# A decoder layer on one core: two batches' Silu by Tanh ahead of the last cross softmax, the last batch in halves, context means early, new orders

## The chip, the cores and the metric

The kernel runs on one core of one Trainium2 chip. The metric is device time in microseconds (us) of one execution; a run's time is a little more than the span that the profiler sees. TensorE (PE) multiplies matrices and transposes, VectorE (DVE) and ScalarE (ACT) work on what it leaves in PSUM, GpSimd (POOL) on SBUF alone, and SyncE (SP) issues DMAs. The engines run at the same time and wait for each other by semaphores.

## What is computed

```python
x = x + attn(layernorm(x), Wq, bq, Wk, bk, Wv, bv, Wo, bo)   # causal, 4 KV heads, rope, d = 16
x = x + xattn(layernorm(x), ctx_2048, mask_BxS2_bk0)         # softmax(x @ ctx.T / 16) @ ctx, masked
x = x + ffn(layernorm(x), w_gate_up, w_down)
# ffn: everything is quantised to 255 steps per row and multiplied back
#   gate, up = quantised(x) @ quantised(w_gate_up).T, split in halves of 704
#   h = silu(gate) * up;  y = quantised(h) @ quantised(w_down).T
```

x is 8 batches of 128 tokens with 256 features; the context is 8 x 128 x 256. The reference's einsum of the scores sums over the 4 query heads of a KV head, so the kernel sums the columns of Wq beforehand.

## The kernel before

One batch is one tile of 128 tokens. For each batch j of 8 the steps are small functions, one call a step: `project` (q, k, v in bank `ps_q`), `rotate` and `rotate_sum` (rope, DVE, with `rotate_c` on POOL), `transpose_qk`, `mask_scores` and `scores` (bank group `ps_s`), `max_scores`, `transpose_q_max`, `mask_other_keys` and `score_keys` (scores transposed, with the row maximum folded in), `exp_self` (ACT), `weigh_values` (`ps_y`), `invert_sums`, `normalise_y`, `project_out`, `residual_1`; then the cross attention: `transpose_x1`, `cross_scores` (`ps_x`), `max_cross`, `bias_cross`, `exp_cross`, `transpose_cross_p`, `readout` (`ps_r`), `residual_2`; then the feed-forward part: `quantise_x`, `transpose_x_int`, `gate_product` (8 matmuls of 352 columns into banks 0 and 1 of `ps_s`), `silu_gate` (ACT), `widen_gate` (POOL: times the scales of the up weights), `up_product` (banks 2 and 3), `hidden` (DVE: up times gate), `amax_h`, `scale_h`, `invert_h`, `quantise_h` (ACT), `transpose_h` (`ps_x`), `evacuate_h`, `down` (`ps_y`), `scale_down` (DVE), `add_residual` (POOL; DVE for the last batch) and the store.

Beside the batches there is work that is done once: the mean over the columns of the weights (`mean_w_first`, `centre_w_first`), bias under rope (`sum_bias`, `rope_bias`, DVE), Wo with bias centred (`bias_wo` on PE, `sum_wo`, `mean_wo`, `centre_wo` on DVE), the token means of the context (`mean_ctx`), the quantisation of the weights (`amax_w1`, `amax_w2`, `quantise_w1`, `quantise_w2`), and the transposes of gate, up and down weights by way of bank `ps_r`. The gate weight is kept as an upper and a lower part (`gate_hi`, `gate_lo`), whose sum has full precision. `keep_warm(n)` are n matmuls on zeros whose result nobody reads.

There is no scheduler. Each engine has one list of calls, written out by hand, and runs it in that order; a wait that is not yet met holds back all that follows on that engine. `done(engine, name, j)` waits until semaphore `name` has counted batch j, `bank_free` and `free` wait until a buffer or bank is read out. So a product into the gate banks waits for the Silu of the batch before:

```python
bank_free(pe, "gate_ready", j)      # gate_product(j) waits for silu_gate(j - 1)
```

Silu needs another set of ACT's function tables than Exp, so the list of ACT has every `exp_cross` ahead of the first `silu_gate`.

## Time and profile before

| | us |
|---|---|
| median of 3 runs | 111.41 |
| lowest and highest | 111.39, 113.15 |
| the profiled execution | 111.01 |
| its span | 109.2 |
| PE busy in the span | 96.1 |
| DVE, ACT, POOL busy | 75.5, 64.7, 60.2 |

Times below are us from the start of the span of the profiled execution. Busy time of PE counts modelled ends of matmuls, so that a full PE is not one at its peak. "PEclk" or the granted clock is the share of the full clock of 2.4 GHz that PE was given; 0.50 is its lower level of 1.2 GHz.

### The profile page before, as it was taken

The page shows a single profiled execution, that of the slowest core. Times are in us where ns is not written, and L with a number is a line of the kernel's source. Part 1 is how long each engine was busy: PE and PEld are TensorE (multiplying, and loading weights), DVE is VectorE, ACT ScalarE, POOL GpSimd, SP SyncE. Part 2 cuts the span into 40 slices and gives each one's busy share as a digit, 9 for nine tenths or more (in the row PEclk, how much of TensorE's full clock was granted, in tenths as well). Part 3 has the DMA queues.
Part 4 walks back from the last instruction along what each step waited for, and adds up shares of the span by engine and source line. Part 5 has one row for each costly group of instructions (what it writes and reads, how often), then busy time and mean ns, then how long its engine had stood idle before and what let it go on. Part 6 is the DMA issues. An engine that isn't in the chain of part 4 may idle for free.

```text
span 109.2 us, 2451 instructions
## 1 busy us (share of the span) xinstructions
PE 96.1 (88%) x827; PEld 74.7 (68%) x827; DVE 75.5 (69%) x216; ACT 64.7 (59%) x169; POOL 60.2 (55%) x122
## 2 busy tenths in 40 slices
PE   6998396999999999999999998766799999999850
PEld 4786284799876677687688786445687888865520
DVE  5176939978669695956984846367698868889331
ACT  1300113870859748686668493889877587788620
POOL 6364402999358994135162143255888968765430
PEclk9999959985599999999999999999999999999999
DMA  2999999700000000000000000000000000111212
GB/s 53 382 331 405 417 420 388 230 0 0 0 9 0 0 0 3 6 0 0 0 6 0 0 0 0 9 0 0 0 0 0 0 0 6 51 48 48 96 54 96
DMA packets 4522, 8.35 MB, mean 76 GB/s; under 512 B 349, under 2 KB 3358, under 8 KB 4382
## 3 DMA queue, kind: packets, MB, share of 16 engines
q1 hardware_dynamic: 4206, 7.64, 19.2%
q10 hardware_dynamic: 304, 0.56, 1.4%
q8 instruction: 7, 0.11, 0.5%
q14 instruction: 5, 0.04, 0.1%
HBM read 7.15 MB, written 1.05 MB: 75 GB/s over the span
## 4 chain that ended last, share of the span: by engine, by line
PE 71%; DVE 12%; ACT 6%; DMA 4%; issue 3%; ACTq 1%; DVEq 0%
PE ps_s L447 15%; PE ps_q L295 7%; PE ps_r L281 5%; PE ps_y L486 5%; DMA mask_sb<-in_mask 4%; PE ps_s L343 3%; PE ps_y L363 3%; PE ps_r L390 3%; PE ps_s L319 3%; PE ps_x L379 3%; PE ps_x L474 3%; PE ps_q L303 2%; PE ps_y L355 2%; PE ps_s L330 2%; PE ps_s L314 2%
## 5 line engine op out<-in xcount | busy, mean ns | idle before, releaser
L1029 POOL TENSOR_TENSOR gate_up<-gate,up_row 128x704 f32<-128x704 f32 x8 | 13.6, 1700 | 3.0 <-ACT gate L645 2.9
L255 PE MATMUL ps_s<-warm 128*128 128x256 bf16 x51 | 9.4, 361 | 1.0 <-DVE warm L679 1.0
L1041 POOL TENSOR_SCALAR x_aug<-x2c 128x256 f32<-128x256 f32 x8 | 3.8, 480 | 10.5 <-DVE x2c L832 10.4
L540 ACT ACTIVATE v_pad<-ps_q,r 128x64 f32<-128x64 f32 x8 | 2.5, 314 | 11.9 <-DVE rot L781 11.9
L804 DVE RECIPROCAL y_rsum<-ps_y 128x128 f32<-128x128 f32 x8 | 7.6, 953 | 2.3 <-PE ps_y L358 2.1
L645 ACT ACTIVATE gate<-ps_s,x_scale 128x704 f32<-128x704 f32 x8 | 6.8, 847 | 3.9 <-PE ps_s L447 3.9
L901 DVE SCALAR_TENSOR_TENSOR hid<-ps_s,x_scale,gate_up 128x704 f32<-128x704 f32 x8 | 7.6, 949 | 1.7 <-PE ps_s L447 1.4
L255 PEld LDWEIGHTS ps_s<-warm 128*128 128x128 bf16 x51 | 6.5, 131 | 3.2 <-DVE warm L679 1.0
L447 PE MATMUL ps_s<-gate_hi,x_int_T 128*128 128x352 f32 x32 | 8.4, 343 | 0.0
L1007 POOL TENSOR_TENSOR rot_c<-rot,b_rope 128x128 f32<-128x128 f32 x8 | 3.6, 455 | 8.5 <-DVE rot L781 8.5
L486 PE MATMUL ps_y<-w_T,h_T 128*128 128x256 bf16 (+1 forms) x48 | 7.5, 276 | 0.6 <-DVE ffn L920 0.6
L447 PE MATMUL ps_s<-gate_lo,x_int_T 128*128 128x352 f32 x32 | 7.8, 323 | 0.0
L650 ACT ACTIVATE h_int<-hid,h_inv 128x704 int16<-128x704 f32 x8 | 7.0, 881 | 1.0 <-PE ps_x L474 0.8
L799 DVE TENSOR_REDUCE qk_rot<-ps_s 128x4 f32<-128x512 f32 x8 | 5.5, 690 | 2.7 <-PE ps_s L319 2.7
L1056 POOL TENSOR_TENSOR y_out<-ffn,x_aug 128x256 f32<-128x256 f32 x7 | 4.8, 690 | 4.4 <-DVE ffn L920 4.4
L781 DVE TENSOR_TENSOR rot<-ps_q,rope_r 128x256 f32<-128x256 f32 x8 | 3.4, 422 | 5.5 <-PE ps_q L295 5.3
L906 DVE TENSOR_REDUCE h_amax<-hid 128x1 f32<-128x704 f32 x8 | 7.0, 876 | 0.1
L920 DVE SCALAR_TENSOR_TENSOR ffn<-ps_y,h_scale,w_row 128x256 f32<-128x256 f32 x8 | 3.9, 482 | 4.5 <-PE ps_y L486 4.3
L447 PE MATMUL ps_s<-up_int,x_int_T 128*128 128x352 f32 x32 | 7.0, 339 | 0.0
L390 PE MATMUL ps_r<-ctx_aug,p_cross_T 128*128 128x257 f32 x16 | 5.2, 407 | 1.6 <-ACT x_int_T L631 0.7
L638 ACT CAST h_T<-ps_x 128x640 bf16<-128x640 int16 x8 | 5.5, 685 | 1.7 <-PE ps_x L474 1.7
L486 PEld LDWEIGHTS ps_y<-w_T,h_T 128*128 128x128 bf16 (+1 forms) x48 | 4.0, 97 | 3.4 <-issue 1.7
(165 smaller groups left out, 282.2 us busy)
## 6 DMA issues: line engine op xcount, KB each, us to landing
w_raw<-in_w SPq DMA_DIRECT2D x2, 512.0 KB, 9.5
ctxT<-in_ctxT SPq DMA_DIRECT2D x1, 1024.0 KB, 12.3
ctx_aug<-in_ctx SPq DMA_DIRECT2D x1, 1024.0 KB, 15.6
out_x<-y_out SPq DMA_DIRECT2D x8, 128.0 KB, 1.7
x_aug<-in_x SPq DMA_DIRECT2D x1, 768.0 KB, 7.4
xT<-in_xT SPq DMA_DIRECT2D x1, 768.0 KB, 8.6
w_raw<-in_w SPq DMA_DIRECT2D x1, 704.0 KB, 13.6
x_first<-in_x_first ACTq DMA_DIRECT2D x1, 416.0 KB, 5.6
```

Of the source, the lines that this page charges most:

```text
L255: nc.tensor.matmul(ps_s[:, H - 1, 0:2 * T], warm[:, 0:P], warm[:, :], start=True, stop=True)
L295: last = nc.tensor.matmul(ps_q[:, 0:6 * QK], x_feature(j, c), wqkv_c[:, c, :, :], start=c == 0, stop=c == DC - 1)
L390: nc.tensor.matmul(ps_r[:, 0:DA], p_cross_T[:, j, :], ctx_aug[:, j, :], start=True, stop=True).then_inc(s["readout_done"], 1)
L447: last = nc.tensor.matmul(ps_s[:, first + i, 0:FH], x_int_T[:, j, c, :], w[:, c, i * FH:(i + 1) * FH], start=c == 0 and w is parts[0], sto ...
L486: last = nc.tensor.matmul(ps_y[:, 0:D], h_T[j % 2][0:n, f, :], w2_T[0:n, f, :], start=f == 0, stop=f == FC - 1)
L638: nc.scalar.copy(h_T[j % 2][:, 0:FC - 1, :], src[:, 0:(FC - 1) * T].rearrange("p (f t) -> p f t", t=T))
L645: nc.scalar.activation(gate[j % 2][:, :, :], ps_s[:, 0:2, 0:FH], ACT.Silu, scale=x_scale[:, j:j + 1]).then_inc(s["gate_ready"], 1)
L650: nc.scalar.mul(h_int[j % 2][:, :], hid[j % 2][:, :, :].rearrange("p i f -> p (i f)"), h_inv[:, j:j + 1]).then_inc(s["h_int_ready"], 1)
L804: nc.vector.reciprocal(y_rsum[j % 3][:, :], ps_ys).then_inc(s["y_rsum_done"], 1)
L901: nc.vector.scalar_tensor_tensor(hid[j % 2][:, :, :], ps_s[:, 2:4, 0:FH], x_scale[:, j:j + 1], gate_up[j % 2][:, :, :], ALU.mult, ALU.mult ...
L906: nc.vector.tensor_reduce(h_amax[:, j:j + 1], hid[j % 2][:, :, :].rearrange("p i f -> p (i f)"), AX.X, ALU.max, apply_absolute_value=True) ...
L1029: nc.gpsimd.tensor_tensor(gate_up[j % 2][:, :, :], gate[j % 2][:, :, :], up_row[:, :].rearrange("p (i f) -> p i f", i=2), ALU.mult).then_i ...
```

## The change

**Silu by Tanh.** For batches 0 and 1 (`EARLY = 2`) silu(g) is computed as g/2 · (1 + tanh(g/2)): ACT takes the tanh from the gate bank (`tanh_gate`), DVE adds 1 and multiplies by the bank (`finish_gate`), and `hidden` uses the scale squared and halved (`x_square`), which POOL computes with `x_half`. A gate product waits for what reads its bank for the batch before: `finish_gate` (batches 0 and 1) or the Silu, which now counts from batch 2 (`gate_free`). **Last batch in halves.** Gate product, Silu, widening (now DVE), `hidden`, maximum, quantisation, transposes, evacuation and `down` of batch 7 go by halves (columns 0 to 351 and the rest for the first steps, 384 and 320 for the quantised ones). The other transposes of h alternate between banks `ps_x` and `ps_q`. **Context means.** `ctxT` is loaded before `xT` and w1; `mean_ctx` comes before the first keys are scored, and each of its 16 matmuls writes 60 equal columns in place of 1 (`CM = 61`). **Elsewhere.** The bias goes to POOL (the key bias is copied by ACT), Wo's centring to ACT, `x_first` is loaded by SP and `wo` by ACT. All four lists of calls are written in another order; that the diff shows only in a line or two of each.

```diff
             sp.dma_start(w_first[:, :], w_first_in).then_inc(s["w_first_loaded"], 16)
+            sp.dma_start(x_first[:, :], x_first_in).then_inc(s["x_first_loaded"], 16)
             sp.dma_start(x_second[:, :], x_second_in).then_inc(s["x_second_loaded"], 16)
-            sp.dma_start(wo_raw[:, :], wo_in).then_inc(s["wo_loaded"], 16)
             sp.dma_start(x_aug[:, 2:B, 0:D], x_in).then_inc(s["x_loaded"], 16)
+            sp.dma_start(ctxT[:, :, :, :], ctxT_in).then_inc(s["ctxT_loaded"], 16)
             sp.dma_start(xT[:, :, :, :], xT_in).then_inc(s["xT_loaded"], 16)
             for part, (first, last) in enumerate(W1_PARTS):
                 sp.dma_start(w1_raw[:, first:last, :], w1_in[:, first:last]).then_inc(s[f"w1_{part}_loaded"], 16)
-            sp.dma_start(ctxT[:, :, :, :], ctxT_in).then_inc(s["ctxT_loaded"], 16)
...
-                    nc.tensor.matmul(ps_s[:, H - 1, 0:2 * T], warm[:, 0:P], warm[:, :], start=True, stop=True)
+                    nc.tensor.matmul(ps_r[:, 0:2 * T], warm[:, 0:P], warm[:, :], start=True, stop=True)
...
+                means = ps_r[:, 0:B * CM].rearrange("p (b n) -> p b n", n=CM)
+                nc.tensor.matmul(means[:, :, 0], mean_w[0:B, :], any_diag[:, :], start=True, stop=True)
                 pe.wait_ge(s["ctxT_loaded"], 16)
                 for j in range(B):
                     for c in range(DC):
-                        last = nc.tensor.matmul(ps_r[:, B + j:B + j + 1], ctxT[:, j, c, :], mean_w[:, 0:1],
+                        last = nc.tensor.matmul(means[:, j, 1:CM], ctxT[:, j, c, :], mean_w[:, 1:CM],
                                                 start=c == 0, stop=c == DC - 1)
                 last.then_inc(s["ctx_mean_done"], 1)
...
+            def gate_free(j):
+
+                if 1 <= j <= EARLY:
+                    pe.wait_ge(s["early_gate_ready"], j)
+                elif j > EARLY:
+                    pe.wait_ge(s["gate_ready"], j - EARLY)
+
             def gate_product(j):
                 if j == 0:
                     done(pe, "p_T_ready", B - 1)
                     done(pe, "gate_lo_ready", 2)
-                bank_free(pe, "gate_ready", j)
+                gate_free(j)
...
+            def last_gate(i):
+
+                if i == 0:
+                    gate_free(LAST)
+                    done(pe, "x_int_T_ready", LAST)
+                for c in range(DC):
+                    for w in (gate_hi, gate_lo):
+                        last = nc.tensor.matmul(ps_s[:, i, 0:FH], x_int_T[:, LAST, c, :], w[:, c, i * FH:(i + 1) * FH],
+                                                start=c == 0 and w is gate_hi, stop=c == DC - 1 and w is gate_lo)
+                last.then_inc(s["last_gate_done"], 1)
...
             def transpose_h(j):
+
+                bank = (ps_x, ps_q)[j % 2]
                 if j == 0:
                     done(pe, "cross_p_T_ready", B - 1)
-                bank_free(pe, "h_T_ready", j)
+                elif j == 1:
+                    done(pe, "qk_T_ready", B - 1)
+                free(pe, "h_T_ready", j, 2)
                 done(pe, "h_int_ready", j)
```

```diff
+            def last_down_a():
+
+                done(pe, "ffn_ready", LAST - 1)
+                done(pe, "last_h_T_a_ready", 0)
+                for f in range(FC // 2):
+                    nc.tensor.matmul(ps_y[:, 0:D], h_T[LAST % 2][:, f, :], w2_T[:, f, :], start=f == 0, stop=False)
+
+            def last_down_b():
+
+                done(pe, "last_h_T_b_ready", 0)
+                for f in range(FC // 2, FC):
+                    n = P if f < FC - 1 else FL
+                    last = nc.tensor.matmul(ps_y[:, 0:D], h_T[LAST % 2][0:n, f, :], w2_T[0:n, f, :],
+                                            start=False, stop=f == FC - 1)
+                last.then_inc(s["down_done"], 1)
...
-            keep_warm(30); mean_w_first(); keep_warm(6); project(0); bias_wo(); keep_warm(10); transpose_qk(0)
-            keep_warm(5); project(1); mask_scores(0); scores(0); transpose_q_max(0); mask_other_keys(0)
...
+            keep_warm(30); mean_w_first(); keep_warm(6); mask_scores(0); bias_wo(); keep_warm(4); project(0)
+            keep_warm(11); transpose_qk(0); project(1); scores(0); keep_warm(7); mean_ctx(None, 0)
+            transpose_q_max(0); mask_other_keys(0); score_keys(0); transpose_qk(1); project(2)
...
+            def copy_key_bias():
+                act.wait_ge(s["x_first_loaded"], 16)
+                nc.scalar.copy(b_qk[:, :, QK:2 * QK], b_raw[:, :, QK * G:]).then_inc(s["bias_copied"], 1)
+
+            def centre_wo():
+
+                done(act, "wo_biased", 0)
+                nc.scalar.activation(y_out[:, 0, :], ps_y[:, 0:D], ACT.Identity, scale=-1.0 / D, accum_out=wo_negmean[:, :]).then_inc(s["wo_summed"], 1)
+                done(act, "wo_summed", 0)
+                nc.scalar.activation(wo_aug[:, 0:D], ps_y[:, 0:D], ACT.Identity, bias=wo_negmean[:, 0:1])
+                nc.scalar.mul(wo_aug[:, D:DA], wo_negmean[:, :], -1.0).then_inc(s["wo_ready"], 1)
...
+            def tanh_gate(j):
+
+                done(act, "x_half_ready", j)
+                done(act, "gate_done", j)
+                nc.scalar.activation(gate[j % 2][:, :, :], ps_s[:, 0:2, 0:FH], ACT.Tanh, scale=x_half[:, j:j + 1]).then_inc(s["tanh_done"], 1)
...
+            def last_silu(i):
+                done(act, "gate_up_ready", LAST - 2)
+                done(act, "x_scale_ready", LAST)
+                done(act, "last_gate_done", i)
+                nc.scalar.activation(gate[LAST % 2][:, i, :], ps_s[:, i, 0:FH], ACT.Silu, scale=x_scale[:, LAST:B]).then_inc(s["last_gate_ready"], 1)
```

```diff
+            def finish_gate(j):
+
+                done(dve, "tanh_done", j)
+                nc.vector.scalar_tensor_tensor(gate[j % 2][:, :, :], gate[j % 2][:, :, :], 1.0, ps_s[:, 0:2, 0:FH],
+                                               ALU.add, ALU.mult).then_inc(s["early_gate_ready"], 1)
+
+            def last_widen(i):
+
+                done(dve, "hid_ready", LAST - 2)
+                done(dve, "last_gate_ready", i)
+                nc.vector.tensor_tensor(gate_up[LAST % 2][:, i, :], gate[LAST % 2][:, i, :], up_row[:, i * FH:(i + 1) * FH],
+                                        ALU.mult).then_inc(s["last_gate_up_ready"], 1)
+
+            def last_hidden(i):
+                done(dve, "h_int_ready", LAST - 2)
+                done(dve, "up_done", LAST)
+                done(dve, "last_gate_up_ready", i)
+                nc.vector.scalar_tensor_tensor(hid[LAST % 2][:, i, :], ps_s[:, 2 + i, 0:FH], x_scale[:, LAST:B], gate_up[LAST % 2][:, i, :],
+                                               ALU.mult, ALU.mult).then_inc(s["last_hid_ready"], 1)
+
+            def last_amax_h(i):
+                done(dve, "last_hid_ready", i)
+                nc.vector.tensor_reduce(last_amax[:, i:i + 1], hid[LAST % 2][:, i, :], AX.X, ALU.max,
+                                        apply_absolute_value=True).then_inc(s["last_amax_done"], 1)
+
...
+                if j < EARLY:
+                    done(dve, "x_square_ready", j)
+                scale = x_square[:, j:j + 1] if j < EARLY else x_scale[:, j:j + 1]
+                nc.vector.scalar_tensor_tensor(hid[j % 2][:, :, :], ps_s[:, 2:4, 0:FH], scale, gate_up[j % 2][:, :, :],
...
-            sum_bias(); rope_bias(); rope_bias_sum(); centre_w_first(); stats_1(1); aggregate_1(1, 2)
-            sum_wo(); mean_wo(); centre_wo(); rotate(0); stats_1(2); exclude(); rotate_sum(0); stats_1(3)
...
+            finish_gate(0); invert_sums(7); residual_2(5); amax_x(5); normalise_y(7); step_x(5); invert_x(5)
+            max_cross(6); bias_cross(6); finish_gate(1); residual_1(7); hidden(0); amax_h(0)
+            scale_h(0); invert_h(0); max_cross(7); bias_cross(7); invert_cross_sum(6); hidden(1); residual_2(6)
```

```diff
+            def sum_bias():
+
+                pool.wait_ge(s["x_first_loaded"], 16)
+                nc.gpsimd.tensor_tensor(bq_half[:, :, :, :], bq_raw[:, :, :, 0:2], bq_raw[:, :, :, 2:4], ALU.add).then_inc(s["bias_half_summed"], 1)
+                done(pool, "bias_half_summed", 0)
+                nc.gpsimd.tensor_tensor(b_qk[:, :, 0:QK], bq_half[:, :, :, 0], bq_half[:, :, :, 1], ALU.add).then_inc(s["bias_summed"], 1)
+
+            def rope_bias():
+                done(pool, "bias_summed", 0)
+                done(pool, "bias_copied", 0)
+                nc.gpsimd.tensor_tensor(b_cos[:, :, :], b_qk[:, :, :], rope_sb[:, 0:2, :], ALU.mult).then_inc(s["b_cos_done"], 1)
+                nc.gpsimd.tensor_tensor(b_sin[:, :, :], b_qk[:, ::-1, :], rope_sb[:, 3:1:-1, :], ALU.mult).then_inc(s["b_sin_done"], 1)
+                done(pool, "b_cos_done", 0)
+                done(pool, "b_sin_done", 0)
+                nc.gpsimd.tensor_tensor(b_rope[:, :, :], b_cos[:, :, :], b_sin[:, :, :], ALU.add).then_inc(s["b_rope_ready"], 1)
...
+                if j < EARLY:
+                    done(pool, "early_gate_ready", j)
+                else:
+                    done(pool, "gate_ready", j - EARLY)
...
+                    done(pool, "x_scale_ready", j)
+                    nc.gpsimd.tensor_scalar(x_half[:, j:j + 1], x_scale[:, j:j + 1], 0.5, 1.0, ALU.mult, ALU.mult).then_inc(s["x_half_ready"], 1)
+                    nc.gpsimd.tensor_scalar(x_square[:, j:j + 1], x_scale[:, j:j + 1], x_scale[:, j:j + 1], 0.5, ALU.mult, ALU.mult).then_inc(s["x_square_ready"], 1)
```

**Order on PE at the context means.** First before: `weigh_values(0)` (two rows), `scores(1)`, the means (`ps_r<-mean_w,ctxT`) and `transpose_q_max(1)` (`ps_s<-ident,qk_rot`) with what follows it.

```order
L355 MATMUL ps_y<-p_self_T,v_pad 32x128 x4
L358 MATMUL ps_y<-p_self_T,ones 32x128 x4
L319 MATMUL ps_s<-qk_T 128x128 x4
L277 MATMUL ps_r<-any_diag,mean_w 128x8
L281 MATMUL ps_r<-mean_w,ctxT 128x1 x16
L325 MATMUL ps_s<-ident,qk_rot 128x128
L330 MATMUL ps_s<-causal_T,ident_b 128x128 x3
L303 MATMUL ps_q<-ident,qk_rot 128x128 x2
```

Now, from `project(1)` and `scores(0)` (`ps_s<-qk_T`) on:

```order
L304 MATMUL ps_q<-wqkv_c,x_second 128x192 x2
L328 MATMUL ps_s<-qk_T 128x128 x4
L263 MATMUL ps_r<-warm 128x256 x7
L286 MATMUL ps_r<-any_diag,mean_w 128x8
L290 MATMUL ps_r<-mean_w,ctxT 128x60 x16
L334 MATMUL ps_s<-ident,qk_rot 128x128
L339 MATMUL ps_s<-causal_T,ident_b 128x128 x4
L352 MATMUL ps_s<-q_max_T,qk_T 128x128 x4
L312 MATMUL ps_q<-ident,qk_rot 128x128 x2
```

The means moved up by one batch, from ahead of `transpose_q_max(1)` to ahead of `transpose_q_max(0)`, behind seven warm matmuls.

**Order on PE at the last cross steps.** `gate_hi`, `gate_lo`, `up_int` are products of the feed-forward part, `ps_x<-ctxT,x1c_T` is `cross_scores`, `ps_r<-ctx_aug,p_cross_T` a `readout`. Before, from `project_out(7)` to the last `transpose_cross_p`:

```order
L363 MATMUL ps_y<-wo_aug,y_T 128x257
L410 MATMUL ps_r<-ident_b,w_int 128x128 x6
L384 MATMUL ps_x<-ident,p_cross 128x128
L390 MATMUL ps_r<-ctx_aug,p_cross_T 128x257
L369 MATMUL ps_x<-ident,x1c 128x128 x2
L447 MATMUL ps_s<-up_int,x_int_T 128x352 x4
L377 MATMUL ps_x<-excluded,ident_b 128x128
L379 MATMUL ps_x<-ctxT,x1c_T 128x128 x2
L438 MATMUL ps_r<-ident_b,x_int 128x128 x2
L390 MATMUL ps_r<-ctx_aug,p_cross_T 128x257
L384 MATMUL ps_x<-ident,p_cross 128x128
```

Now, the same stretch, from `project_out(7)` on:

```order
L372 MATMUL ps_y<-wo_aug,y_T 128x257
L393 MATMUL ps_x<-ident,p_cross 128x128
L447 MATMUL ps_r<-ident_b,x_int 128x128 x2
L378 MATMUL ps_x<-ident,x1c 128x128 x2
L456 MATMUL ps_s<-gate_hi,x_int_T 128x352 x2
L456 MATMUL ps_s<-gate_lo,x_int_T 128x352 x2
L456 MATMUL ps_s<-gate_hi,x_int_T 128x352 x2
L456 MATMUL ps_s<-gate_lo,x_int_T 128x352 x2
L386 MATMUL ps_x<-excluded,ident_b 128x128
L388 MATMUL ps_x<-ctxT,x1c_T 128x128 x2
L456 MATMUL ps_s<-up_int,x_int_T 128x352 x4
L399 MATMUL ps_r<-ctx_aug,p_cross_T 128x257
```

`gate_product(2)` and `up_product(1)` now stand here, and `gate_product(1)` and `up_product(0)` ahead of the first row; before, `gate_product(1)` and all that follow it stood behind the last `transpose_cross_p`.

**Order on ACT there.** Before, the last `exp_cross` (`p_cross,c_sum`), the table load and the first Silu (`gate<-ps_s,x_scale`):

```order
L627 ACTIVATE x_int<-x2c,x_inv 128x256
L631 CAST x_int_T<-ps_r 128x256
L573 ACTIVATE p_cross,c_sum<-ps_x,c_bias,c_scale 128x128
L645 ACT_TABLE_LOAD
L645 ACTIVATE gate<-ps_s,x_scale 128x704
L578 COPY p_cross_T<-ps_x 128x128
L582 ACTIVATE y_out,x_sumsq<-x2c 128x256
```

Now, with the two Tanh (`gate<-ps_s,x_half`) among the cross exponentials, and the table load:

```order
L641 ACTIVATE p_cross,c_sum<-ps_x,c_bias,c_scale 128x128
L732 ACTIVATE gate<-ps_s,x_half 128x704
L646 COPY p_cross_T<-ps_x 128x128
L679 CAST up_int<-ps_r 128x3x2x128
...
L732 ACTIVATE gate<-ps_s,x_half 128x704
L641 ACTIVATE p_cross,c_sum<-ps_x,c_bias,c_scale 128x128
...
L749 ACTIVATE h_int<-hid,h_inv 128x704
L641 ACTIVATE p_cross,c_sum<-ps_x,c_bias,c_scale 128x128
L738 ACT_TABLE_LOAD
L738 ACTIVATE gate<-ps_s,x_scale 128x704
```

The Tanh of batches 0 and 1 stand ahead of `exp_cross(6)`; no table load stands between them and the exponentials. The first Silu, still behind the last `exp_cross`, is that of batch 2.

**Order on DVE at the end.** Before, from `hidden(7)` on:

```order
L901 SCALAR_TENSOR_TENSOR hid<-ps_s,x_scale,gate_up 128x704
L920 SCALAR_TENSOR_TENSOR ffn<-ps_y,h_scale,w_row 128x256
L906 TENSOR_REDUCE h_amax<-hid 128x1
L911 TENSOR_SCALAR h_scale<-h_amax 128x1
L915 RECIPROCAL h_inv<-h_scale 128x1
L920 SCALAR_TENSOR_TENSOR ffn<-ps_y,h_scale,w_row 128x256 x4
L927 TENSOR_TENSOR y_out<-ffn,x_aug 128x256
```

Now, from `last_widen(0)` on:

```order
L986 TENSOR_TENSOR gate_up<-gate,up_row 128x352 x2
L993 SCALAR_TENSOR_TENSOR hid<-ps_s,x_scale,gate_up 128x352
L1040 SCALAR_TENSOR_TENSOR ffn<-ps_y,h_scale,w_row 128x256
L993 SCALAR_TENSOR_TENSOR hid<-ps_s,x_scale,gate_up 128x352
L998 TENSOR_REDUCE last_amax<-hid 128x1 x2
L1040 SCALAR_TENSOR_TENSOR ffn<-ps_y,h_scale,w_row 128x256
L1003 TENSOR_SCALAR h_amax<-last_amax 128x1
L1031 TENSOR_SCALAR h_scale<-h_amax 128x1
L1035 RECIPROCAL h_inv<-h_scale 128x1
L1040 SCALAR_TENSOR_TENSOR ffn<-ps_y,h_scale,w_row 128x256
L1009 CAST h_T<-ps_r 128x256
```

The steps of batch 7 are in two pieces, and three of the last four `scale_down` stand between them.

## Rows read from the trace of the kernel before

**Rows 1.** Windows: busy us (instructions) of each engine, granted clock, DMA share, GB/s

```profile
13.24:16.43 3.19, 3.19 (x15) 2.67 (x15) 1.35 (x5) 0.37 (x1) 0.00 (x0) 0.51 1.04 432
21.63:23.78 2.15, 2.15 (x20) 2.15 (x19) 1.44 (x4) 1.86 (x6) 2.15 (x6) 0.95 0.00 0
23.78:26.75 2.97, 2.97 (x16) 2.97 (x16) 2.64 (x6) 0.28 (x1) 2.97 (x7) 0.50 0.00 0
26.75:30.50 3.75, 3.75 (x22) 3.12 (x22) 2.03 (x4) 2.32 (x6) 1.59 (x4) 0.51 0.00 0
31.90:63.61 31.71, 30.96 (x359) 23.68 (x355) 24.17 (x70) 22.92 (x76) 16.13 (x39) 1.00 0.01 2
63.61:80.28 16.67, 12.84 (x95) 10.01 (x96) 9.75 (x32) 13.12 (x38) 9.05 (x18) 1.00 0.01 1
80.28:98.03 17.75, 17.75 (x129) 14.57 (x128) 14.81 (x32) 13.48 (x23) 14.05 (x16) 1.00 0.05 16
98.03:109.20 11.17, 6.74 (x55) 3.90 (x52) 5.22 (x13) 4.95 (x11) 3.46 (x5) 0.99 0.21 72
```

**Rows 2.** Timeline of PE: start, us, instruction, idle time before it

```profile
9.12 0.89 PE L295 MATMUL ps_q<-wqkv_c,x_first 128*128 128x192 f32 x4 [0.49 <-DVE wqkv_c L723]
...
13.24 0.65 PE L303 MATMUL ps_q<-ident,qk_rot 128*128 128x128 f32 x2 [1.70 <-DVE qk_rot L791]
...
21.63 5.26 PE L281 MATMUL ps_r<-mean_w,ctxT 128*128 128x1 f32 x32
```

**Rows 3.** Timeline of DVE in the first 28 us

```profile
11.53 0.41 DVE L781 TENSOR_TENSOR rot<-ps_q,rope_r 128x256 f32<-128x256 f32 x1
...
17.29 0.69 DVE L799 TENSOR_REDUCE qk_rot<-ps_s 128x4 f32<-128x512 f32 x1 [0.20 <-PE ps_s L319]
...
23.43 0.49 DVE L791 TENSOR_TENSOR qk_rot<-rot_c,rot 128x128 f32<-128x128 f32 x1 [0.71 <-POOL rot_c L1007]
...
26.23 0.26 DVE L808 TENSOR_TENSOR y_T<-ps_y,y_rsum 128x128 f32<-128x128 f32 x1
...
27.02 1.61 DVE L878 TENSOR_REDUCE w_amax<-w_raw 128x2 f32<-128x1408 f32 x1
```

**Rows 4.** Page, DMA issues: KB each, us from issue to landing

```profile
w_raw<-in_w SPq DMA_DIRECT2D x2, 512.0 KB, 9.5
ctxT<-in_ctxT SPq DMA_DIRECT2D x1, 1024.0 KB, 12.3
```

**Rows 5.** Timeline of the SP queue, the issue of `ctxT`

```profile
4.99 0.50 SPq L235 DMA_DIRECT2D ctxT<-in_ctxT  x1
```

**Rows 6.** Timeline of ACT at the first Silu

```profile
73.02 1.28 ACT L645 ACT_TABLE_LOAD   x1
74.32 0.85 ACT L645 ACTIVATE gate<-ps_s,x_scale 128x704 f32<-128x704 f32 x1
```

**Rows 7.** Groups by form: count, busy us and mean ns, idle before

```profile
L901 DVE SCALAR_TENSOR_TENSOR hid<-ps_s,x_scale,gate_up 128x704 f32<-128x704 f32 x8 | 7.6, 949 | 1.7 <-PE ps_s L447 1.4 <-ACT h_int L650 0.2
...
L1007 POOL TENSOR_TENSOR rot_c<-rot,b_rope 128x128 f32<-128x128 f32 x8 | 3.6, 455 | 8.5 <-DVE rot L781 8.5
...
L871 DVE TENSOR_TENSOR gate_lo<-ps_r,gate_hi 128x256 fp32r<-128x256 f32 x5 | 1.9, 416 | 0.1
```

**Rows 8.** Chain that ended last, pieces in order of time: start, us, what

```profile
39.38 0.43 PE ps_y L363 x2
39.82 0.44 PE ps_r L399 x4
...
98.03 0.47 PE ps_x L474 x6
98.50 0.88 PE ps_y L486 x6
...
99.96 0.80 DVE h_amax L906
...
101.23 0.56 ACT h_int L650
```

268 lines of the change are left out of this document (146 added, 122 removed).

## The prediction

> **What bounds the kernel now.** Read first TensorE's (PE's) busy time and granted clock by stretch [rows 1]. Time lies in five places. The head, up to 21.63 us, is one chain through all engines. From 21.63 to 30.5 PE is always busy, but from 23.78 on its clock stands at 0.50, the lower level (1.2 GHz). From 31.9 to 63.61 (end of `scores(2)` to start of `gate_product(0)`) PE works 30.96 of 31.71 us at 2.4 GHz: PE is the bound. From 63.61 to 80.28 it works 12.84 of 16.67 us: 3.83 us idle, the last batches' cross softmax. From 80.28 to 98.03 it is full again. The last 11.17 us are the chain of the last batch.
>
> Then read why. The 32 passes of the context means (`mean_ctx`) fill 21.63 to 26.89 [rows 2]. The clock fell in the middle of them and was back only at 30.5. Earlier, PE idled 1.70 us for `qk_rot` and then ran 13.24 to 16.43 at 0.51 [rows 1, 2]. In the head VectorE (DVE) is in the way: `project(0)` ends at 10.01, `rot` starts only at 11.53, since bias and Wo work stand ahead of it [rows 2, 3]. At the far end the first Silu waits behind the last cross exponential and a table load of 1.28 us [rows 6]. `gate_product(1)` can't overwrite its bank before that Silu ends, at 75.2, although `gate_product(0)` began at 63.61.
>
> **The change part by part.** All times are of the profiled execution, 109.20 us of span, 111.01 us in all; the median of the runs is 111.41. Forecasts below are added to 111.01.
>
> *Loads.* `ctxT` is issued at 4.99 and lands 12.3 us later, at 17.3 [rows 4, 5]. It moves ahead of `xT` and three parts of w1, 2,176 KB. At the 432 GB/s of that time [rows 1] this is 5.2 us, so it lands near 12.1. The means want it at 14.3 (below), so 2.2 us of slack. w1 in turn lands 2.5 us later (1,024 KB): its first part, issued before `ctxT` and 9.5 us on the way [rows 4], near 15.5; DVE wants it at about 15.6. That is no slack: a late transfer would cost its lateness, up to 1 us.
>
> *Head up to the means.* PE's queue now has `mask_scores(0)`, `bias_wo` and four warm matmuls ahead of `project(0)`, an estimated 1.2 us (four of six bf16 transposes at 0.47, a projection's 0.43, four of the six 256-column matmuls at 0.88, each share rounded [rows 8]). PE was free at 8.63 [rows 2], so `project(0)` ends near 10.6, not 10.01. But DVE is free: bias goes to GpSimd (POOL), Wo to ScalarE (ACT). Five POOL operations of at most 0.46 us [rows 7] take 2.3 us, ready near 9.9, before `rotate_c(0)` can ask at 11.0: hidden, with 1 us of cover. `rot` starts at 10.6 instead of 11.53, the transposes at about 12.1 instead of 13.24. The idle time that preceded the clock's fall shrinks from 1.7 to some 0.6 us (11 warm matmuls fill in), so I take `project(1)` and `scores(0)` at 2.4 GHz, ending at 13.5. Seven warm matmuls bring 14.3.
>
> *The means.* 16 matmuls (32 passes) of 1 column become as many of 60. With r the time of a pass at 2.4 GHz, 2.15/r + 2.97/2r = 32 [rows 1], so r = 0.114 us. Four fp32 passes with 128 columns take 0.44 us, 0.11 each [rows 8]: a wider pass costs no more, the weight load paces both. All at the high level: 3.6 us, ending at 18.1 with the small matmul ahead. Bounds: 3.6 us (wider passes aren't shorter) and 5.2 us (60 columns not hidden at all: 60/257 of the 0.215 us pass of `project_out` [rows 8], 32 times, on top). I take 3.6, nearest to the rows. So PE comes to `transpose_q_max(0)` at 18.1, no earlier than before, when `max_scores(0)` ended at 17.98 [rows 3], but with the means behind it.
>
> *From there to the end of `scores(2)`.* Before: 31.9. What is late next is DVE: from `max_scores(0)` at 17.29 to the end of `y_T` at 26.49 it needed 9.2 us with 0.71 us idle [rows 3], 8.5 of work. After, it also has `keep_valid` (16 numbers, an estimated 0.2) and `lower_gate(0)` (two of 0.42 [rows 7]), 9.5 in all, starting at 14.2. It will wait about 1 us for PE and ACT (for `project(2)`, which needs its bank evacuated behind a quantisation on ACT, and for `gate_hi`), so `y_T` of batch 0 is done at 24.7. Then PE has `project_out(0)`, `project(3)`, a gate transpose, mask, `transpose_x1(0)`, `scores(2)`: 2.5 us. That gives 27.2 instead of 31.9: **4.7 us gained**, 3.4 of it the half of 6.72 us at low clock.
>
> *Attention, to `gate_product(0)`.* The order shifts PE work over the borders: away go two gate transposes (0.88), `transpose_x1(0)` (0.22, half of one), `project_out(6)` (0.43), one cross transpose (0.11); added are a readout (0.43, as a projection) and `transpose_up(0)` (six bf16 transposes, 0.47) [rows 8]: −0.74. But `amax_w2` (1.61 us of DVE [rows 3]), once covered by the slow means, now stands ahead of `rotate(3)` and `max_scores(2)`: I add 0.5 us. Stretch 31.5: **0.2 us gained**. At most the whole 1.6 us would show.
>
> *Gates ahead of the last softmax.* Batches 0 and 1 use Tanh on ACT (no row; bounds 0.56 us, the part of a quantisation of these columns that shows in the chain [rows 8], and 0.95, the slowest pass over them [rows 7]; I take the Silu's 0.85 [rows 6], same shape and engine) and one pass on DVE like `hid`, 0.95 [rows 7]. After `gate_product(0)` PE has 2.2 us of other work (`project_out(6)`, cross transpose, `transpose_up(1)`, `weigh_values(7)`, `transpose_x1(6)`, a readout) before it needs the bank again; 0.85 + 0.95 and the waits around them end in about the same time. So `gate_product(1)`, `up_product(0)`, `gate_product(2)`, `up_product(1)` slide in between the cross steps of batches 5 to 7 and fill the 3.83 us. Two extra scalings on POOL are off the path. I expect new idle spots: 0.4 at `transpose_x1(7)` (DVE has `finish_gate(1)` ahead of `residual_1(7)`), 0.25 at the last cross transpose, 0.25 at `gate_product(3)` behind table load and Silu: 0.9. Moved over the border to here: `project_out(6)`, a cross transpose, one more `transpose_h` (0.47) and `down` (0.88), less a readout and `transpose_up(0)`: +0.99. From `gate_product(0)` to the end of `up_product(7)`: 34.42 − 3.83 + 0.99 + 0.9 = 32.5: **1.9 us gained**. Two banks for h transposes take away ACT waits that PE's other work already hides: 0.
>
> Here a rule speaks against it. In the trace the table load starts at 73.02 and the Silu at 74.32 [rows 6]: the switch costs its 1.28 us and nothing visible more. The Trainium skill, "ScalarE: Activation LUTs", section What ACT_TABLE_LOAD costs, counts a drain of about 1.38 us besides. By that figure `gate_product(3)` would wait 1.4 us longer and the sum be 104.3; the trace does not agree, so the row stands.
>
> *The last batch in halves.* Before: 11.17 us from `up_product(7)` to the end. Its chain has maximum (0.80), two small steps, quantisation (0.56 to the queued end), transposes 0.47, evacuation, `down` 0.88, scaling, addition, store [rows 8]. After, by halves: first product ends 0.5 after `up_product(7)`; the second stands behind `scale_down(4)`, which needs two transposes and `down(4)` from PE, 2.3; maxima and `scale_down(5)` 3.7; scales 4.2; first half quantised 4.7; second half transposed 5.5, evacuated on DVE 6.2; rest of down 6.7; scaled and added 7.8; the store as before, 2.1 (from the last addition's end at 107.1 to 109.2). Sum 9.9: **1.2 us gained**. Bounds: 2 us (no waits for the other batches' downs) and 0 (seven more fixed costs eat the halves).
>
> **Sum.** 4.7 + 0.2 + 1.9 + 1.2 = 8.0; 111.01 − 8.0 = **103.0 us**.
>
> **Rivals.** (a) *The clock falls in the means again.* For it: the means are still narrow passes, like those under which it fell. Against: before, they ran 1 column and the clock still held for 2.15 us. Price: the 3.4 us come back, to 106.4; some of it hides under the DVE wait, 106.0. Chance 0.14. (b) *The slack is larger than I see*: the 1 us wait at `y_T`, the 0.5 for `amax_w2` and the 0.9 idle don't appear: 100.6. For it: DVE works only 24.17 of 31.71 us in the attention stretch. Chance 0.18. (c) *DVE takes PE's place at the cross steps*: 1.9 us of `finish_gate` and the earlier `hid` passes stand in its queue ahead of `max_cross(7)`. Then the 1.9 us are not gained: 104.9. Chance 0.10. (d) *Slower.* One mechanism: the low clock level, once fallen in the means, is held through the early attention steps, which now have DVE waits in them. Each us of PE work there costs one more; to eat 8.0 us it has to last 16 us beyond what I sum, up to about 35 us, and 20 us to be slower by over 2%: 113.5. Against: from 26.75 to 30.5 dense PE work brought it back [rows 1]. Chance 0.02. (e) *Tanh doesn't share Exp's tables*, and the sets are switched: three more loads of 1.28 us on ACT amid cross steps, 106.8. Against: after the one at the start, ACT's order has a single load, before the first Silu. Chance 0.01. The rest, 0.55, is the forecast.
>
> **How the numbers follow.** Case (b) at 100.6 and (a) at 106.0 lie inside the range if it goes from 99.8 to 106.5; the bounds of w1's landing, `amax_w2` and the last batch (1 us each) are within. About 2% is what a measurement of this kernel can tell from no change; 2% under 111.41 is 109.2. Every case but (d) lies below: faster 0.94. Of the rest, part of (d) and the unforeseen, 0.04 within 2% and 0.02 slower.
>
> **What would show it.** Granted clock 1.00 from 14 to 30 us, the means in about 3.6 us (else (a)); `rot` of batch 0 near 10.6; end of `scores(2)` near 27; `gate_product(0)` near 59 and `gate_product(1)` less than 3.5 us after its end, with no PE gap over 0.5 us up to `gate_product(3)` (else (c)); one table load after the last cross exponential; about 10 us from the last `up_product` to the end. The prediction is wrong if PE has long waits between 14 and 30 us, for w1 or for DVE, or if the last exponential comes later than 70 us.

## The result, and the profile after

The changed kernel takes 102.12 us (median of 4 runs, 101.38 to 102.22) where the kernel before took 111.40 beside it (111.09 to 113.15): a ratio of 0.9175, interval 0.9118 to 0.9232. The forecast was 103.0. The profiled execution has a span of 100.4 us, its time is 102.22. Repeated on another chip, the changed kernel came out at 102.35 (101.67 to 102.54) and the kernel before at 110.23 (107.89 to 113.66): a ratio of 0.9306, interval 0.9248 to 0.9364, which doesn't meet the first. Ratios leave out executions more than 1.5% above the fastest of the same kernel in their set; of the kernel before that leaves 20 of the 47 later ones, at 107.89 to 110.63 us, while the profiled execution, from which the rows and the forecast were taken, took 111.01. So the gain is 7 to 9 us, according to the executions of the kernel before that it is told from. The changed kernel's own time is the steadier base: differences below are told from 102.12 us in runs 1 and 3 and the first attempt of run 2, and from 102.35 in the rest, unless it is said otherwise.

The page after, PE and its granted clock in 40 slices of 2.5 us:

```profile
PE   5999699989999999999999999998999999999560
PEclk9999999999999999999999999999999999999995
```

The clock is at its high level (2.4 GHz) until PE has hardly anything left to do, in the last slice. Windows of the changed kernel, which answer to [rows 1]; columns as there:

```profile
12.66:15.20 2.54, 2.54 (x22) 1.91 (x22) 1.88 (x7) 0.31 (x1) 1.51 (x4) 1.00 1.02 406
15.20:18.91 3.71, 3.71 (x34) 3.70 (x35) 3.35 (x13) 0.00 (x0) 2.20 (x4) 1.00 1.03 391
18.91:22.50 3.59, 2.94 (x28) 2.04 (x26) 1.80 (x5) 2.96 (x8) 1.71 (x4) 1.00 0.57 186
22.50:28.42 5.92, 5.62 (x70) 4.25 (x68) 5.37 (x10) 5.81 (x18) 5.13 (x12) 1.00 0.02 4
28.42:58.10 29.68, 29.44 (x354) 22.84 (x351) 23.96 (x71) 22.24 (x74) 18.31 (x45) 1.00 0.01 2
58.10:72.00 13.90, 13.39 (x97) 10.57 (x98) 11.83 (x31) 11.79 (x32) 8.13 (x16) 1.00 0.01 2
72.00:90.12 18.12, 18.12 (x133) 14.66 (x132) 15.12 (x40) 14.60 (x31) 14.71 (x20) 1.00 0.06 19
90.12:100.40 10.28, 5.57 (x43) 2.96 (x40) 5.65 (x16) 3.92 (x9) 2.09 (x3) 0.89 0.20 70
```

Borders: 28.42 is the end of `scores(2)` (before 31.9), 58.10 the start of `gate_product(0)` (63.61), 90.12 the end of `up_product(7)` (98.03). So 3.5 us were gained up to the first border, 2.0 in attention (31.71 to 29.68), 2.4 in the gates' stretch (34.42 to 32.02) and 0.9 in the tail (11.17 to 10.28): 8.8 in all, the two spans' 109.2 − 100.4. The stretches don't hold quite the same work, since steps moved over the borders.

**Head.** PE's timeline, which answers to [rows 2]: what remains are short waits.

```profile
15.12 3.78 PE L290 MATMUL ps_r<-mean_w,ctxT 128*128 128x60 f32 x32
18.74 0.28 PE L334 MATMUL ps_s<-ident,qk_rot 128*128 128x128 f32 x1
...
20.88 0.92 PE L304 MATMUL ps_q<-wqkv_c,xT 128*128 128x192 f32 x4 [0.46 <-ACT qk_T L614]
...
25.82 0.70 PE L372 MATMUL ps_y<-wo_aug,y_T 128*128 128x257 f32 x2 [0.17 <-DVE y_T L888]
```

The means, 5.26 us before, take 3.7. The timeline of ACT shows who waits for them: `q_max` of batch 0 is transposed behind them, and ACT stands still for 4.61 us.

```profile
19.06 0.27 ACT L620 COPY q_max_T<-ps_s 128x128 f32<-128x128 f32 x1 [4.61 <-PE ps_s L334]
```

**Last cross steps.** Timeline of PE, ACT and DVE from the second gate on (answers to [rows 6]):

```profile
61.71 0.67 PE L456 MATMUL ps_s<-gate_hi,x_int_T 128*128 128x352 f32 x2
...
63.44 0.85 ACT L732 ACTIVATE gate<-ps_s,x_half 128x704 f32<-128x704 f32 x1 [0.66 <-PE ps_s L456]
...
64.48 0.88 DVE L979 SCALAR_TENSOR_TENSOR gate<-gate,ps_s 128x704 f32<-128x704 f32 x1
64.60 0.46 ACT L641 ACTIVATE p_cross<-ps_x,c_bias,c_scale 128x128 f32<-128x128 f32 x1 [0.31 <-DVE c_bias L903]
...
69.47 1.28 ACT L738 ACT_TABLE_LOAD   x1
69.50 0.33 PE L393 MATMUL ps_x<-ident,p_cross 128*128 128x128 f32 x1 [0.23 <-ACT p_cross L641]
70.76 0.85 ACT L738 ACTIVATE gate<-ps_s,x_scale 128x704 f32<-128x704 f32 x1
```

A Tanh (0.85 us) is followed by a cross exponential without a table load; the only load after the one at the start stands behind the last exponential, under PE's other work. The longest PE wait left there is the 0.23 us at 69.50. The Silu follows the load's end at once, so the drain that the Trainium skill, "ScalarE: Activation LUTs", section What ACT_TABLE_LOAD costs, puts beside the load is not seen here either.

**Tail.** Timeline of DVE, ACT and PE in the last 10 us (answers to the end of [rows 8]):

```profile
90.73 0.57 DVE L993 SCALAR_TENSOR_TENSOR hid<-ps_s,x_scale,gate_up 128x352 f32<-128x352 f32 x1
91.56 0.48 DVE L1040 SCALAR_TENSOR_TENSOR ffn<-ps_y,h_scale,w_row 128x256 f32<-128x256 f32 x1 [0.26 <-PE ps_y L538]
...
91.96 0.57 DVE L993 SCALAR_TENSOR_TENSOR hid<-ps_s,x_scale,gate_up 128x352 f32<-128x352 f32 x1
...
92.45 0.93 DVE L998 TENSOR_REDUCE last_amax<-hid 128x1 f32<-128x352 f32 x2
...
93.84 0.93 PE L538 MATMUL ps_y<-w_T,h_T 128*128 128x256 bf16 x6 [0.80 <-DVE ffn L1040]
...
94.38 1.07 ACT L755 ACTIVATE h_int<-hid,h_inv 128x384 int16<-128x384 f32 x2 [1.43 <-DVE h_inv L1035]
```

Both halves of `hid` stand around a `scale_down` that waits for PE, and `down(6)` waits 0.80 us for the next one. But `down(6)` is done at 94.77, before the first half of `h_int` has been transposed. The chain that ended last runs by ACT there, which quantises the first half and later evacuates its transposes:

```profile
94.38 0.62 ACT h_int L755
...
95.56 0.49 ACT h_T L725
```

Both halves of the last `down` follow that evacuation, from 96.18 to 97.23.

### The profile page after: what moved, and what is told of

The parts are those of the page before. It is cut to its first block, busy times and chain, and to the rows that moved or that the text cites. A ratio compares the mean times of both kernels' runs of the same rounds, so it can differ in the third digit from the quotient of the medians.

```text
span 100.4 us, 2487 instructions
## 1 busy us (share of the span) xinstructions
PE 92.1 (92%) x834; PEld 71.3 (71%) x834; DVE 75.4 (75%) x217; ACT 65.1 (65%) x175; POOL 61.5 (61%) x130
## 4 chain that ended last, share of the span: by engine, by line
PE 72%; DVE 13%; POOL 6%; issue 3%; ACT 3%; DVEq 0%; ACTq 0%; POOLq 0%
PE ps_s L456 11%; PE ps_r L263 8%; PE ps_q L304 6%; PE ps_y L538 4%; PE ps_r L290 4%; PE ps_y L372 3%; POOL gate_up L1169 3%; PE ps_r L399 3%; PE ps_s L352 3%; PE ps_s L328 3%; PE ps_x L388 2%; PE ps_q L312 2%; PE ps_y L364 2%; PE ps_s L339 2%; PE ps_s L482 2%
## 5 line engine op out<-in xcount | busy, mean ns | idle before, releaser
L1169 POOL TENSOR_TENSOR gate_up<-gate,up_row 128x704 f32<-128x704 f32 x7 | 11.9, 1699 | 6.6 <-ACT gate L738 5.0
L263 PE MATMUL ps_r<-warm 128*128 128x256 bf16 x58 | 9.5, 330 | 1.0 <-DVE warm L786 1.0
L263 PEld LDWEIGHTS ps_r<-warm 128*128 128x128 bf16 x58 | 6.7, 120 | 3.1 <-DVE warm L786 1.0
L620 ACT COPY q_max_T<-ps_s 128x128 f32<-128x128 f32 x8 | 2.1, 265 | 6.2 <-PE ps_s L334 5.9
L1021 DVE SCALAR_TENSOR_TENSOR hid<-ps_s,x_scale,gate_up 128x704 f32<-128x704 f32 x5 | 4.8, 951 | 1.8 <-PE ps_s L456 1.2
L738 ACT ACTIVATE gate<-ps_s,x_scale 128x704 f32<-128x704 f32 x5 | 4.2, 847 | 2.3 <-PE ps_s L456 2.3
L304 PE MATMUL ps_q<-wqkv_c,xT 128*128 128x192 f32 x24 | 5.3, 341 | 0.5 <-ACT qk_T L614 0.5
L625 ACT ACTIVATE p_self_T<-ps_s 128x512 f32<-128x512 f32 x8 | 4.8, 596 | 1.4 <-PE ps_s L352 1.3
L1175 POOL TENSOR_SCALAR ctx_aug<-ctx_aug,valid_mean,ctx_negmean 128x256 f32<-128x256 f32 x8 | 4.4, 549 | 1.7 <-DVE ctx_negmean L853 1.7
L456 PEld LDWEIGHTS ps_s<-up_int,x_int_T 128*128 128x128 f32 x32 | 5.2, 189 | 0.2 <-DVE hid L1021 0.2
## 6 DMA issues: line engine op xcount, KB each, us to landing
w_raw<-in_w SPq DMA_DIRECT2D x1, 704.0 KB, 14.8
```

The source lines that it names most:

```text
L263: nc.tensor.matmul(ps_r[:, 0:2 * T], warm[:, 0:P], warm[:, :], start=True, stop=True)
L304: last = nc.tensor.matmul(ps_q[:, 0:6 * QK], x_feature(j, c), wqkv_c[:, c, :, :], start=c == 0, stop=c == DC - 1)
L456: last = nc.tensor.matmul(ps_s[:, first + i, 0:FH], x_int_T[:, j, c, :], w[:, c, i * FH:(i + 1) * FH], start=c == 0 and w is parts[0], sto ...
L625: nc.scalar.activation(p_self_T[j % 3][:, :, :], ps_s[:, :, 0:T], ACT.Exp).then_inc(s["p_T_ready"], 1)
L1021: nc.vector.scalar_tensor_tensor(hid[j % 2][:, :, :], ps_s[:, 2:4, 0:FH], scale, gate_up[j % 2][:, :, :], ALU.mult, ALU.mult).then_inc(s[" ...
L1169: nc.gpsimd.tensor_tensor(gate_up[j % 2][:, :, :], gate[j % 2][:, :, :], up_row[:, :].rearrange("p (i f) -> p i f", i=2), ALU.mult).then_i ...
```

## The experiments

Eleven kernels, and the changed one once more, ran in four sets, each set on one chip. "Changed" is the kernel above. The changed kernel as it is ran beside experiments 4, 5 and the first order of 7.

**1. The columns of the means.** Back to one column:

```diff
-    CM = 61
+    CM = 2
```

> The changed kernel with each context-mean matmul writing 1 column again, at its new place behind seven warm matmuls. Theory (the wide columns hold the clock): the granted clock falls to 0.50 during the means or just behind them, they take over 4.5 us instead of 3.71, and the time rises by 2.0 to 3.4 us, to about 104.5. Rival (the early place and the denser work around it hold the clock, the columns do nothing): clock 1.00 throughout, time within 0.3 us of 102.1.

Measured: 104.25 us (103.80 to 104.67), ratio to before 0.9527 (0.9455 to 0.9598), 2.1 us above the changed kernel. The means in PE's timeline, and windows from them on:

```profile
14.71 3.73 PE L290 MATMUL ps_r<-mean_w,ctxT 128*128 128x1 f32 x32
...
15.00:18.50 3.50, 3.50 (x33) 3.49 (x34) 3.27 (x11) 0.00 (x0) 2.21 (x4) 1.00 1.02 395
18.50:19.00 0.50, 0.31 (x5) 0.14 (x3) 0.50 (x2) 0.35 (x2) 0.00 (x0) 0.70 1.09 375
19.00:25.00 6.00, 5.54 (x39) 4.20 (x43) 2.05 (x7) 3.77 (x10) 3.25 (x7) 0.50 0.35 115
```

The means are no faster with one column (3.7 us both), so 59 more columns are free. But behind them the clock drops to its low level for some 6 us. It fell behind the means and not in them, so they didn't take the 4.5 us of the theory; the time is within its range. The wide columns pay by the clock alone.

The same one edit made alone in the kernel before:

```diff
-                    ... ps_r[:, B + j:B + j + 1], ctxT[:, j, c, :], mean_w[:, 0:1],
+                    ... means[:, j, 1:CM], ctxT[:, j, c, :], mean_w[:, 1:CM],
```

> The kernel before, changed in one thing: the means write 60 columns each. Theory (the clock alone): the clock stays at 1.00 from 21.6 to 30.5, the means take 3.7 us instead of 5.26, and 2.5 to 3.4 us are gained, to about 108.5. Rival (a wait for DVE takes over at once, since its queue has 8.5 us of work up to y_T and the weight maxima behind it): under 1.5 us gained, over 109.9. Third: the clock falls all the same, no gain.

Measured: 107.17 us (106.55 to 108.34), ratio 0.9775 (0.9700 to 0.9851), 2.5 us less than the before of its set. The medians of the runs in the ratio, 106.96 and 109.27, are 2.3 apart. Its PE timeline:

```profile
13.56 0.44 PE L305 MATMUL ps_q<-ident,qk_rot 128*128 128x128 f32 x2 [1.70 <-DVE qk_rot L794]
...
20.51 3.78 PE L283 MATMUL ps_r<-mean_w,ctxT 128*128 128x60 f32 x32
...
27.44 0.50 PE L321 MATMUL ps_s<-qk_T 16*128 16x128 f32 x8
```

The granted clock is 1.00 from 10 to 95 us, and `scores(2)` ends at 27.94 instead of 31.9. Not all of these 4.0 us are the columns' doing. The means begin 1.1 us sooner (20.51 and 21.63), ahead of all that the edit touches: in this execution the clock held behind the 1.70 us wait for `qk_rot`, where it stood at 0.51 behind the same wait in the profiled one of the kernel before [rows 1]. By the ratio the columns are worth 2.3 to 2.5 us, a third of the 7 us between the two kernels in the later sets. It is one number in the code.

A second thing can be read here. The old order with wide columns ends `scores(2)` at 27.94, the changed kernel at 28.42, with two gate transposes and `transpose_x1(0)` more behind it, 1.1 us at the prediction's prices. So beyond the clock, the new order and places of work in the head are worth some 0.6 us, an estimate from these rows.

**2. The last batch in one piece.** First attempt, the nine steps of the last batch that go by halves replaced by whole ones (of DVE's list one line is shown):

```diff
-last_widen(1); last_hidden(0); scale_down(4); last_hidden(1); last_amax_h(0); last_amax_h(1)
+scale_down(4); hidden(7); amax_h(7)
```

> The changed kernel with the last batch in one piece: one gate product, Silu, widening on POOL, product, maximum, quantisation, six transposes, one down. Theory (halves are worth about 1 us): from the end of the last up product to the end of the span 11.2 to 12 us instead of 10.28, time 103.1 to 103.9. Rival (the fixed cost of the extra steps eats the halves): within 0.3 us of 102.1.

Measured: 104.56 us (104.08 to 105.34), ratio 0.9563 (0.9482 to 0.9643), 2.4 us above the changed kernel. But its DVE row shows a fault of the new order, not of the whole batch: `hidden(7)` stands behind a `scale_down` that waits for POOL, where `widen_gate(7)` stood ahead of the addition that frees the buffer.

```profile
91.80 0.48 DVE L1040 SCALAR_TENSOR_TENSOR ffn<-ps_y,h_scale,w_row 128x256 f32<-128x256 f32 x1 [1.84 <-POOL y_out L1200]
```

So it was run again with the order that the kernel before has there:

```diff
-scale_down(4); hidden(7); amax_h(7)
+hidden(7); scale_down(4); amax_h(7)
```

> The changed kernel with the last batch in one piece again, as in the run before on this, but with the neighbours ordered as the kernel before has them: hidden(7) stands ahead of scale_down(4) on VectorE, and widen_gate(7) behind add_residual(2) on GpSimd. In the earlier run hidden(7) stood behind a scale_down that waited 1.84 us for GpSimd. Theory (the halves are worth 1.2 us, as forecast from the chain of the last batch): 1.0 to 1.6 us slower than the changed kernel, with about 11.3 us from the end of up_product(7) to the end. Rival (halving is worth all of the 2.2 us that the earlier run showed): 2 to 2.5 us slower. Second rival (halving is worth under half a microsecond, the rest is order): 0.5 us slower at most.

Measured: 103.1 us by the three runs of the ratio (103.0, 103.1 and 104.03; the other three took 105.07 to 105.33), ratio 0.9503 (0.9403 to 0.9604). Their spans are 101.2 to 101.3. The span of 101.2 stands 0.8 above the changed kernel's 100.4. The same rows of two profiled executions can lie half a microsecond apart from the start on; a second one of the changed kernel has `up_product(7)` at 88.79 where this run has it at 88.72, and a span of 100.2. So this part of the change is worth 0.8 to 1.0 us of span, 0.75 of the time (103.1 against 102.35), not 2.4: between the theory's 1.0 to 1.6 and the second rival's 0.5. It isn't the halves alone, for the run also gives the widening back to POOL, and DVE waits for it:

```profile
90.94 0.95 DVE L1021 SCALAR_TENSOR_TENSOR hid<-ps_s,x_scale,gate_up 128x704 f32<-128x704 f32 x1 [1.30 <-POOL gate_up L1169]
```

Halves and engine were not tried apart.

**3. Silu in Tanh's place.** Batches 0 and 1 by Silu, without `finish_gate`:

```diff
-ACT.Tanh, scale=x_half[:, j:j + 1]
+ACT.Silu, scale=x_scale[:, j:j + 1]
```

> The changed kernel with Silu at the place of the two Tanh, without the two finishing passes on DVE; ACT must then load tables before the first Silu, before the next cross exponential and before the third Silu: two loads of 1.28 us more, 1.8 us of DVE less. Theory (the new order is the gain, Tanh saves only loads that would stand in ACT's queue at the last cross steps): 1 to 2 us slower, 103.1 to 104.1. Rival (ACT has slack there, DVE is tighter): within 0.4 us or faster.

Measured: 104.95 us (104.64 to 105.52), ratio 0.9608 (0.9529 to 0.9688), 2.8 us above the changed kernel. Its ACT timeline has three loads where the changed kernel has one (both have another at the start):

```profile
59.16 1.28 ACT L732 ACT_TABLE_LOAD   x1 [0.25 <-PE ps_s L456]
...
65.18 1.28 ACT L641 ACT_TABLE_LOAD   x1
...
71.32 1.28 ACT L738 ACT_TABLE_LOAD   x1
```

PE works 11.28 us of the window 58.10 to 72.00, not 13.39: 2.1 us of new idle time, and 2.5 us more of span. Two loads are 2.6 us; nearly all of that reaches the end, although DVE has 1.8 us less to do. The theory's 1 to 2 us was too little.

**4. The gates behind the last softmax.** No Tanh, `gate_product(1)`, `gate_product(2)` and `up_product(1)` behind `transpose_cross_p(7)`, the other engines' gate work in step:

```diff
-readout(5, "up_int_ready", 1); gate_product(1); cross_scores(6); up_product(0)
+readout(5, "up_int_ready", 1); cross_scores(6); up_product(0)
...
-transpose_x1(7); gate_product(2); cross_scores(7)
-up_product(1); readout(6, ...); transpose_cross_p(7); up_product(2)
+transpose_x1(7); cross_scores(7); readout(6, ...); transpose_cross_p(7)
+gate_product(1); up_product(1); gate_product(2); up_product(2)
```

> The changed kernel without tanh: gate_product(1), gate_product(2) and up_product(1) stand behind transpose_cross_p(7), all gates are Silu, and the gates' work on the other engines stands behind exp_cross(7). It keeps every other part. Theory (TensorE waited in the last cross steps of the kernel before, and the two early gates fill that): TensorE's idle time between gate_product(0) and transpose_cross_p(7) rises from 0.25 us to 2 to 4 us, and the kernel is 2 to 4 us slower than the changed one. Rival (the gain of this stretch comes from the order and the masks rather than from the early gates): under 1 us slower.

Measured: 110.01 us (109.80 to 110.38), ratio 1.0046 (1.0018 to 1.0074): 7.7 us above the changed kernel, twice what the theory allowed. Its windows:

```profile
58.10:64.00 5.90, 5.46 (x49) 3.99 (x47) 4.09 (x16) 3.24 (x11) 2.80 (x9) 1.00 0.01 3
64.00:68.50 4.50, 2.98 (x12) 1.73 (x12) 0.92 (x5) 3.10 (x12) 1.42 (x4) 0.79 0.01 2
68.50:77.00 8.50, 6.32 (x20) 5.57 (x21) 3.19 (x7) 4.69 (x9) 3.38 (x2) 0.51 0.00 0
77.00:98.00 21.00, 20.85 (x152) 16.64 (x151) 17.41 (x43) 15.77 (x30) 15.01 (x20) 1.00 0.06 20
```

PE is idle for 4.3 us of these 39.9, against 0.5 in the changed kernel's stretch: 3.8 us, as the theory had it. The rest is clock in this trace: 6.32 us of work at 0.51 would be 3.2 at full speed, and part of the 2.98 at 0.79 goes the same way, some 3.7 us. The split is shown for this execution alone. All ten of the kernel have spans of 107.9 to 108.2 us, while their mean clocks go from 0.931 to 0.974 (0.934 here), so a higher clock did not shorten the others; what took its place no trace shows. The kernel before has the same 3.83 us of idle time there [rows 1] at a clock of 1.00. So this run doesn't say that the early gates are worth 7.7 us against the kernel before; it says that an order with the same idle time in fewer, longer pieces (up to 1.69 us here, 0.71 there) can cost double.

**5. Bias and Wo back on VectorE.**

```diff
-sum_wq(); copy_ident(); centre_w_first(); stats_1(1)
-aggregate_1(1, 2); find_valid(); rotate(0)
+sum_wq(); copy_ident(); sum_bias(); rope_bias(); rope_bias_sum(); centre_w_first(); stats_1(1)
+aggregate_1(1, 2); find_valid(); sum_wo(); mean_wo(); centre_wo(); rotate(0)
```

> The changed kernel with the bias sums of the rotary part and the means of Wo back on VectorE, ahead of rotate(0), as in the kernel before. Theory (the head was paced by VectorE ahead of rotate(0)): rotate(0) starts at 11.3 to 11.6 instead of 10.26, the transposes of qk(0) at 12.9 to 13.2 instead of 11.76, and the whole kernel is 0.8 to 1.3 us slower than the changed one. Rival (the loads of the context and w1 set the means and all behind them, so that the earlier rotation only lengthens the wait there): 0.3 us slower at most, since the seven keep_warm matmuls have 0.9 us of room.

Beside it ran the changed kernel unaltered:

> The changed kernel itself once more, as it is, so that the four kernels of this set can be compared with it on the same chip: expected at 0.917 of the kernel before (interval 0.912 to 0.923 in the first measurement), with a span near 100.4 us.

Measured: 102.34 us (102.01 to 103.34) and 102.35 (101.67 to 102.54); ratios 0.9331 (0.9245 to 0.9418) and 0.9306 (0.9248 to 0.9364). No difference: the theory fell. DVE's timeline, first in the experiment, then in the kernel before:

```profile
9.22 0.42 DVE L839 TENSOR_REDUCE wo_sum<-ps_y 128x1 f32<-128x256 f32 x1
...
10.38 0.42 DVE L877 TENSOR_TENSOR rot<-ps_q,rope_r 128x256 f32<-128x256 f32 x1
```

```profile
10.48 0.42 DVE L744 TENSOR_REDUCE wo_sum<-ps_y 128x1 f32<-128x256 f32 x1 [0.95 <-PE ps_y L271]
```

With the work back on DVE, `rot` starts at 10.38, not at 11.53. What had held it was that `sum_wo` waited 0.95 us for PE's `bias_wo`, which stood behind `project(0)`, and the rotation behind `sum_wo`. PE's order cured it, not the change of engine. The rival, that an early rotation only lengthens a later wait, wasn't tested, since the rotation stayed early.

**6. The amax of w2 twice.**

```diff
+done(dve, "w2_amax_done", 0)
+nc.vector.tensor_reduce(w2_amax[:, :], w2_raw[:, :, :], AX.X, ALU.max, ...)
```

> The changed kernel with the amax of w2 on VectorE done twice in a row: 1.61 us more of VectorE work at 28.5 us, ahead of rotate(3) and max_scores(2), and nothing else. Its first pass costs TensorE 0.21 us of waiting at 29.4 in the changed kernel, where 0.5 was forecast and 1.6 was the bound. Theory (VectorE is at the edge there: TensorE waits for the rotated q and k of the next batch at once, and what TensorE loses it can't give back, since it is busy to the end): 1.3 to 1.8 us slower than the changed kernel. Rival (VectorE works only 23.96 of 29.68 us in the attention steps and has room): 0.3 us slower at most.

Measured: 105.82 us (105.50 to 106.02), ratio 0.9708 (0.9650 to 0.9765): 3.5 us above the changed kernel for 1.62 us of DVE work. PE's row, and then the windows around it:

```profile
31.61 0.33 PE L334 MATMUL ps_s<-ident,qk_rot 128*128 128x128 f32 x1 [1.87 <-DVE qk_rot L879]
```

```profile
31.60:33.00 1.40, 1.36 (x16) 0.93 (x16) 1.31 (x4) 1.01 (x3) 0.74 (x2) 1.00 0.02 6
33.00:36.50 3.50, 3.50 (x19) 2.77 (x19) 1.97 (x10) 2.35 (x7) 0.82 (x2) 0.54 0.00 0
36.50:58.10 21.60, 21.60 (x254) 16.76 (x250) 17.52 (x51) 15.26 (x52) 14.09 (x35) 1.00 0.01 2
```

The wait grew from 0.21 to 1.87 us, and from 33.0 on the clock stood at 0.54 for 3.5 us, another 1.6 lost: 3.3 in all, the difference of the two spans (103.7 and 100.4). DVE has no room at this spot although it works only 23.96 of 29.68 us of the stretch.

**7. The means later.** Three orders that put ACT's 4.61 idle us to use. First, the means behind `project(2)`:

```diff
-scores(0); keep_warm(7); mean_ctx(None, 0)
-transpose_q_max(0); mask_other_keys(0); score_keys(0); transpose_qk(1); project(2)
+scores(0); keep_warm(8)
+transpose_q_max(0); mask_other_keys(0); transpose_qk(1); score_keys(0); project(2); mean_ctx(None, 0)
```

> The changed kernel with the 32 mean matmuls behind the transpose of q_max(0), both masks, the transposes of qk(1), the scores on the keys and the projection of batch 2, and with ScalarE, VectorE and GpSimd in the order that fits. In the changed kernel ScalarE has 4.61 us of idle time ahead of evacuate_q_max(0) and VectorE 1.51 us ahead of rotate(2), both for want of what TensorE does behind the means. Theory (the means stand too early, and the head is paid for by the two idle engines): evacuate_q_max(0) starts near 15.4 instead of 19.06, the end of scores(2) comes 1 to 1.6 us sooner, and so does the end of the kernel: 0.5 to 1.6 us less than the changed kernel. Rival (the quantisation of Wgate waits for w1_inv, which needs the amax of w1, which needs the loads; y_T of batch 0 needs them in the end): the idle time moves from ScalarE to VectorE, and the time is the same within 0.3 us. Second rival: work of lower_gate and keep_valid now ends later and holds gate product and cross steps: 0.5 us or more slower.

Measured: 102.91 us (102.07 to 104.39), ratio 0.9359 (0.9283 to 0.9435), no gain. In the profiled execution, the longest of the six, PE waits 1.46 us for `gate_lo` ahead of 24.65, and the clock is low from about 26.5 to 29.9. Then behind `weigh_values(0)` too:

```diff
+scores(1); weigh_values(0); mean_ctx(None, 0); transpose_q_max(1); mask_other_keys(1)
+transpose_gate(0, "valid_ready", 0); transpose_qk(2); score_keys(1); project_out(0); project(3)
```

> The changed kernel with the 32 mean matmuls behind weigh_values(0), and so behind everything of TensorE that batch 0 needs up to y_T; the gate transposes follow them. VectorE rotates batch 2 and finishes y_T of batch 0 ahead of the last amax of w1. In the changed kernel TensorE is idle for 0.95 us between the means and the end of scores(2) at 28.42, for want of rotated q and k, q_max and y_T. Theory (the place of the means makes these waits): y_T of batch 0 is done at 21 to 22 instead of 25.76, the end of scores(2) comes 0.7 to 1.2 us sooner, and the kernel is 0.5 to 1.2 us faster than the changed one. Rival (the gate transposes and lower_gate, now late and close together, make new waits of the same size): within 0.3 us, or slower when TensorE's clock falls over a wait of more than a microsecond, as with the means placed a little later (there it waited 1.46 us for gate_lo, and the clock stood at 0.84 from 22.5 to 28.4).

Measured: 103.30 us (102.42 to 103.98), ratio 0.9459 (0.9391 to 0.9526), 1.0 us above the changed kernel. Timeline of DVE and PE:

```profile
21.68 0.29 DVE L888 TENSOR_TENSOR y_T<-ps_y,y_rsum 128x128 f32<-128x128 f32 x1
...
24.67 0.70 PE L372 MATMUL ps_y<-wo_aug,y_T 128*128 128x257 f32 x2
...
27.93 0.66 PE L408 MATMUL ps_r<-ident,w_q 128*128 128x128 f32 x4 [1.47 <-DVE gate_lo L951]
```

`y_T` is early by 3.8 us as expected, and PE gives it back in one wait between two gate transposes, which share a bank. Last, these spread out:

```diff
-project(3); transpose_gate(1, ...); transpose_gate(2, ...); mask_scores(2); ... weigh_values(1)
+transpose_gate(1, ...); project(3); mask_scores(2); ... weigh_values(1); transpose_gate(2, ...)
```

> The run before on this with the three gate transposes spread out: the second stands ahead of project(3), the third behind weigh_values(1), with evacuate_x1(0) ahead of upper_gate(2) on ScalarE, and the amax of w2 ahead of lower_gate(1) on VectorE. The run before on this had y_T of batch 0 at 21.97 us instead of 25.76, and TensorE lost it again in one wait of 1.47 us for gate_lo behind the second gate transpose. Theory (that wait was the whole of the loss): it goes, TensorE's idle time from 15.2 us to the end of scores(2) falls from 1.6 us to under 0.5, and the time is 101.2 to 101.8 us, 0.5 to 1.0 below the changed kernel's 102.1 to 102.4. Rival (VectorE has so much of the gates, w1 and w2 to do there that the wait only turns into one for the rotated q and k of batch 2, behind the amax of w2): TensorE waits for qk_rot at 29 to 30 us, and the time is within 0.3 us of the changed kernel's, or above.

Measured: 102.20 us (101.46 to 102.67), ratio 0.9300 (0.9236 to 0.9364): the changed kernel's time. Two rows of PE:

```profile
27.38 0.43 PE L364 MATMUL ps_y<-p_self_T,v_pad 128*32 128x128 f32 x8
...
30.66 0.23 PE L339 MATMUL ps_s<-causal_T,ident_b 128*128 128x128 bf16 x1 [0.43 <-ACT q_max_T L620]
```

`scores(2)` now ends at 27.4, 1.0 us sooner, but half of that is the gate transpose moved behind it, and the rest goes in new waits: 0.21 for `gate_lo`, 0.43 for `q_max_T`, one more warm matmul ahead. From there on the two kernels run level: the Tanh of batch 0 starts at 59.56 and 59.60, `down(6)` at 93.84 in both. The rival held in substance, though the wait for `qk_rot` that it named didn't come: the price isn't in ACT's idle time. In the changed kernel PE is idle for 1.2 us in all from 15.20 to 58.10, and PE alone sets the end.

## Why the prediction held, step by step

- **Clock in the means** (3.4 of the 4.7 us): the mechanism was right, shown by run 1 from both sides; the size was too large, 2.1 us by the one kernel and 2.3 to 2.5 by the other. Pass time 0.114, 3.6 us forecast, 3.71 measured. Rival (a) would have come true with one column, at 104.25 rather than 106.0, since the fall comes behind the means and ends sooner.
- **Head, 4.7 forecast, 3.5 measured.** The term that was mis-sized is the time ahead of the means: with the small matmul in front they began at 14.8, not 14.3, and ended at 18.9, not 18.1, although `rot` and the transposes came 0.3 us earlier than forecast. A PE wait of 0.46 us for `qk_T` on ACT ahead of `project(1)` had no place in the sum, nor had a second one ahead of `project(2)`. From there on the forecast ran nearly parallel: `y_T` done at 25.76 instead of 24.7, `scores(2)` at 28.42 instead of 27.2. Of the 3.5 us, 1.1 were already lost ahead of the means in the profiled execution of the kernel before and not in another of the same old order (run 1). The loads held: `ctxT` landed at 11.5 (12.1 forecast), and DVE took w1 at 15.57 without waiting.
- **"In the head VectorE is in the way"**: the time of `rot` was right (10.6 forecast, 10.26 measured), the reason wrong (run 5). It was a wait of DVE for PE, in front of which I had read only DVE's own work.
- **Attention, 31.5 forecast, 29.68 measured.** The work moved over the borders was 1.5 us rather than 0.74 (PE busy 30.96 and 29.44), and the idle time fell from 0.75 to 0.24 instead of staying. For `amax_w2` I added 0.5; it cost 0.21. Rival (b) described this stretch, and no other. "At most the whole 1.6 us would show" was too kind a bound: 1.62 us more cost 3.5 (run 6).
- **Gates, 32.5 forecast, 32.02 measured**: right, with 0.5 us of PE idle time instead of 0.9. `gate_product(1)` came at 61.71, 2.2 us after `gate_product(0)`'s end. Rival (e), that Tanh brings its own tables, is refuted by the rows; run 3 shows the price of two loads there, 2.5 to 2.8 us. Rival (c) isn't seen: the wait at the last cross transpose is 0.23 us.
- **Tail, 1.2 forecast, 0.9 measured.** Run 2 puts halves and widening on DVE together at 0.8 to 1.0 us. The forecast held up to the scales (4.2 us behind `up_product(7)`, 4.16 measured). The 0.4 us were lost behind them: ACT's quantisation of the first half showed with 0.62 instead of 0.5 us, and `down` waited for ACT's evacuation of that half, so that it ended at 7.1 instead of 6.7. The 0.80 us wait of `down(6)` is off this chain.
- The terms 4.7, 0.2, 1.9 and 1.2 were measured as 3.5, 2.0, 2.4 and 0.9. The errors partly cancel: 103.0 against 102.1 is nearer than its terms are, and that much is luck. So is the base: the 8.0 us were taken from an execution of 111.01 us, and from 109.2, near the median of those in the later ratios, the same sum would have given 101.2.
- Two sums are slightly off: the shares ahead of `project(0)` add up to 1.3 us, not 1.2 (1.15 measured), and 103.0 with 1.4 more is 104.4, not 104.3.

What stays open: why the clock falls behind a wait in one execution and holds behind an equal one in another (1.70 us in the kernel before and in run 1) wasn't settled. The seven and eleven warm matmuls of the head weren't tried on their own.

## What to carry to other kernels

Where PE is the bound, count its idle time by stretch before moving anything: here 1.2 us were left from 15 to 58 us, and three reorderings of the head won nothing. Price a wait by what the clock may do behind it too: 1.66 us more of one wait cost 3.5. Before taking a base for a forecast, look at how far the runs of the old kernel lie apart, and where the clock was low in the one that was profiled. When an engine seems busy ahead of a step, look at what the last instruction of that work waited for, since a matmul one place too late in PE's queue looks just like an overloaded VectorE.

## What the runs showed of the hardware

- An fp32 matmul with 128 rows and columns of weights took the same time with 1 and with 60 moving columns: 32 passes in 3.7 us, 0.116 us each. Behind 1 column the granted clock fell without any PE wait (run 1, from about 18.7 us, for 6 us); with 60 it stayed at 1.00.
- Work on Tanh between two Exp caused no table load; Silu between two Exp caused two, 1.28 us each.
- The clock fell behind a single PE wait of 1.87 us (run 6) for 3.5 us. In run 4 it fell at 66.5, behind waits of 1.0 and 0.6 us, and stayed low for some 10 us, with waits of 0.4 and 1.7 us in them.
- Equal waits were followed by a fall in one execution and not in another: 1.70 us (low from 13.24 in the kernel before; 1.00 in run 1's second kernel), and 1.46 and 1.47 us (low from about 26.5 in run 7's first order; 1.00 from 22.5 to 58 in its second). The length of the wait alone doesn't settle it.
